# Cross attention over 12,544 keys on one NeuronCore: key splits shared with GpSimd, weights loaded later, and small sums taken off TensorE

## The reference, cut to what matters

```python
# x: (1, 128, 256), ctx: (1, 12544, 256), all fp32
h = layernorm(x)
Sim = (h @ w1)[:, None] + (ctx @ w2)[None, :] + (h * w3) @ ctx.T + b_sim     # 128 x 12544
hq_hat = softmax(Sim, axis=1) @ ctx                                          # 128 x 256
batt = softmax(max(Sim, axis=1), axis=0)                                     # over the 128 tokens
hc_bar = batt @ h                                                            # 256
x = x + concat([h, hq_hat, h * hq_hat, h * hc_bar]) @ W_qv + b_qv
x = x + linear_attention(layernorm(x), Wq, Wk, Wv, Wo, rope)                 # 16 heads, no softmax
x = x + sigmoid(shift_mix(ln(x)) @ W_r) * (relu(shift_mix(ln(x)) @ W_k) ** 2 @ W_v)
```

## Time and profile before

| what | value |
|---|---|
| median of 3 runs | 112.9 us (112.89 to 113.84) |
| the profiled execution's own time | 112.94 us |
| its span, first to last instruction | 111.2 us (1.74 us lie around it) |
| busy in the span | TensorE 105.4 us (95%), VectorE 93.6 (84%), ScalarE 81.3 (73%), GpSimd 26.2 (24%) |
| TensorE's share of the chain of waits | 91% |
| loads | 29.82 MB, nearly all on one queue |
| TensorE clock granted | full (2.4 GHz) in the whole span |

### The profile page before, as it was taken

How to read it: one execution, slowest core, us unless ns; L and a number is a source line. 1 busy time by engine, 2 the same in 40 slices (tenths; PEclk the granted TensorE clock), 3 DMA queues, 4 the chain that set the end, 5 groups by cost and what they waited for, 6 DMA issues and landing times.

```text
span 111.2 us, 1842 instructions
## 1 busy us (share of the span) xinstructions
PE 105.4 (95%) x580; PEld 85.2 (77%) x581; DVE 93.6 (84%) x153; ACT 81.3 (73%) x170; POOL 26.2 (24%) x44
## 2 busy tenths in 40 slices
PE   5899999999999999999999999999999998998890
PEld 2368777676757668888989999898989997887680
DVE  1488999989999999989999999999999846684342
ACT  5076755889979986999999899989986625903450
POOL 2239100000023334124242423367230000100100
PEclk9999999999999999999999999999999999999999
DMA  3999999999999999999999999950000000000001
GB/s 79 382 410 422 420 416 423 420 420 420 410 422 417 420 413 420 422 404 398 439 401 410 422 422 420 414 201 3 3 0 0 0 6 0 0 0 3 6 0 47
DMA packets 8220, 29.82 MB, mean 268 GB/s; under 512 B 1042, under 2 KB 1298, under 8 KB 8082
## 3 DMA queue, kind: packets, MB, share of 16 engines
q1 hardware_dynamic: 8064, 29.69, 66.0%
q10 hardware_dynamic: 146, 0.01, 0.1%
HBM read 29.57 MB, written 0.13 MB: 267 GB/s over the span
## 4 chain that ended last, share of the span: by engine, by line
PE 91%; DVE 2%; DMA 2%; issue 1%; ACT 1%; POOL 1%; DVEq 0%; POOLq 0%; ACTq 0%
PE mixed_ps L988 18%; PE scores_ps L959 10%; PE mixed_ps L990 9%; PE scores_ps L916 9%; PE scores_ps L945 8%; PE scores_ps L931 8%; PE scores_ps L935 8%; PE scores_ps L970 3%; DMA x_sb<-x_dram 2%; PE scores_ps L1081 2%; PE mixed_ps L1133 2%; PE side_ps L1007 1%; PE scores_ps L1146 1%; PE side_ps L1124 1%; PE scores_ps L1007 1%
## 5 line engine op out<-in xcount | busy, mean ns | idle before, releaser
L689 DVE TENSOR_TENSOR pair<-raw,pair 128x1024 fp32r<-128x1024 f32 (+1 forms) x41 | 49.4, 1220 | 1.4 <-ACT pair L486 1.4
L486 ACT ACTIVATE pair<-raw 128x512 fp32r<-128x512 f32 (+1 forms) x41 | 33.3, 814 | 6.6 <-DMA raw<-keys_dram 5.1
L988 PE MATMUL mixed_ps<-pair,turned_high 128*128 128x512 f32 x84 | 32.3, 418 | 0.0
L990 PE MATMUL mixed_ps<-pair,turned_low 128*128 128x256 f32 x84 | 23.6, 281 | 0.0
L461 POOL CAST pair<-raw 128x512 fp32r<-128x512 f32 x22 | 13.6, 618 | 27.2 <-DVE pair L689 23.9
L988 PEld LDWEIGHTS mixed_ps<-pair,turned_high 128*128 128x128 f32 x84 | 15.8, 188 | 2.8
L712 DVE TENSOR_SCALAR_CACHE_REDUCE neg_scores<-scores_ps,neg_max 128x1024 f32<-128x1024 f32 (+2 forms) x14 | 16.0, 1145 | 0.4
L518 ACT ACTIVATE turned_high<-scores_ps 128x512 fp32r<-128x512 f32 (+1 forms) x23 | 13.4, 584 | 3.9 <-PE scores_ps L959 3.9
L990 PEld LDWEIGHTS mixed_ps<-pair,turned_low 128*128 128x128 f32 x84 | 16.0, 190 | 0.0
L719 DVE TENSOR_TENSOR turned_low<-scores_ps,turned_high 128x512 fp32r<-128x512 f32 (+1 forms) x23 | 15.3, 669 | 0.2 <-ACT turned_high L518 0.2
L959 PE MATMUL scores_ps<-ident,neg_scores 128*128 128x128 f32 x98 | 14.6, 272 | 0.0
(11 more groups left out here) (189 smaller groups left out, 129.6 us busy)
## 6 DMA issues: line engine op xcount, KB each, us to landing
raw<-keys_dram SPq DMA_DIRECT2D x24, 512.0 KB, 10.6
raw<-rows_dram SPq DMA_DIRECT2D x24, 512.0 KB, 8.7
w<-weights_dram SPq DMA_DIRECT2D x1, 1792.0 KB, 9.5
w<-weights_dram SPq DMA_DIRECT2D x2, 512.0 KB, 11.5
const<-const_dram SPq DMA_DIRECT2D x1, 832.0 KB, 10.9
raw<-keys_last_dram SPq DMA_DIRECT2D x1, 256.0 KB, 9.5
raw<-rows_last_dram SPq DMA_DIRECT2D x1, 256.0 KB, 6.1
x_sb<-x_dram SPq DMA_DIRECT2D x1, 128.0 KB, 2.3
```

The source lines that it names most:

```text
L486: nc.scalar.activation(pair[:, use % PAIR_BUFS, 0, 0:columns], raw[:, slot(item), 0:columns], ACT.Copy)\
L689: nc.vector.tensor_tensor(out=pair[:, use % PAIR_BUFS, 1, 0:columns], in0=raw[:, slot(item), 0:columns], in1=pair[:, use % PAIR_BUFS, 0, 0 ...
L988: nc.tensor.matmul(mixed_ps[:, :].rearrange("p (h d) -> p h d", h=2), probs_high, both[:, :, t * D:(t + 1) * D], start=(k == EARLY and t = ...
L990: last = nc.tensor.matmul(mixed_ps[:, 0:D], probs_low, rows_tile(high, t), start=False, stop=(k == LATE - 1 and end))
```

## The change

It does the following.

1. Chunk 12 is no longer native, so it is split like the others. Six chunks are shared (10, 12, 14, 18, 20, 22), and in each GpSimd makes the low part of the last 448 of 1024 columns, VectorE that of the first 576.
2. The halves of W_qv are loaded behind chunks 12 and 18. The weight sums and the centring of blocks 0 to 3 come later in ScalarE's list; block 4 to 7's means and centring come after both `early_exp`, ahead of the first rows.
3. Chunks 22 and 23 are taken out of PSUM together.
4. h @ w1 + b_sim: GpSimd multiplies h by w1, loaded as rows (128 KB, behind chunk 13); ScalarE sums it behind the high part of chunk 19; VectorE adds b_sim where it takes the maximum. The three matmul instructions go.
5. Token attention: ScalarE takes the exponential of all 128 spread maxima in every partition and sums it; VectorE makes hc_bar with two multiply-and-sum instructions over 128 columns at k = 10. TensorE's three matmul instructions at k = 8 go.
6. The centred x is transposed by TensorE at the very start, copied out by ScalarE behind the high part of chunk 3, and added on VectorE together with the bias when x1 leaves PSUM, both halves on VectorE. The two instructions of L1065 go.

```diff
 EPS = 1e-5
-NATIVE = (0, 4, 8, 12, 16, 24)
-SHARED = (18, 20, 22)
+NATIVE = (0, 4, 8, 16, 24)
+SHARED = (10, 12, 14, 18, 20, 22)
+POOL_COLUMNS = 448
+W_BEHIND = (12, 18)
...
-    evictions = [(k, k + 1) for k in range(0, CHUNKS - 3, 2)] + [(k,) for k in range(CHUNKS - 3, CHUNKS)]
+    evictions = [(k, k + 1) for k in range(0, CHUNKS - 1, 2)] + [(CHUNKS - 1,)]
     EVICTIONS = len(evictions)
...
                 sp.dma_start(raw[:, slot(k), 0:width_of(k) * DH], src).then_inc(loaded[slot(k)], 16)
-                if k in (8, 11):
-                    part = (k - 8) // 3
+                if k in W_BEHIND:
+                    part = W_BEHIND.index(k)
                     sp.dma_start(w[:, 4 * part:4 * part + 4, :], blocks_in[:, 4 * part:4 * part + 4, :])\
                         .then_inc(w_qv_loaded[part], 16)
+                if k == 13:
+                    sp.dma_start(w1_rows[:, :], w1_rows_in).then_inc(w1_rows_loaded, 16)
             for k in range(CHUNKS):
...
                 use = split_before[k]
+                if k == 18:
+                    pool.wait_ge(low_done, split_before[15] + 1)
+                    pool.wait_ge(normed_done, DH)
+                    pool.wait_ge(w1_rows_loaded, 16)
+                    nc.gpsimd.tensor_tensor(out=hw1_parts, in0=normed[:, :], in1=w1_rows[:, 0:D], op=ALU.mult)\
+                        .then_inc(hw1_multiplied, 1)
                 pool.wait_ge(low_done, split_before[k - 1] + 1)
                 pool.wait_ge(high_done, use + 1)
-                nc.gpsimd.tensor_tensor(out=keys_part(pair[:, use % PAIR_BUFS, 1, :], k, DH - 1),
-                                        in0=keys_part(raw[:, slot(k), :], k, DH - 1),
-                                        in1=keys_part(pair[:, use % PAIR_BUFS, 0, :], k, DH - 1).bitcast(F32),
+                shared = slice(ITEM - POOL_COLUMNS, ITEM)
+                nc.gpsimd.tensor_tensor(out=pair[:, use % PAIR_BUFS, 1, shared], in0=raw[:, slot(k), shared],
+                                        in1=pair[:, use % PAIR_BUFS, 0, shared].bitcast(F32),
                                         op=ALU.subtract).then_inc(pool_low_done, 1)
...
                 act.wait_ge(x_neg_mean_done, 1)
-                nc.scalar.activation(x_c[:, :], x_sb[:, :], ACT.Identity, bias=x_neg_mean[:, :]).then_inc(x_c_done, 1)
-
+                nc.scalar.activation(x_c, x_sb[:, :], ACT.Identity, bias=x_neg_mean[:, :]).then_inc(x_c_done, 1)
+
+            center_x()
             act.wait_ge(q_done, DH)
...
                     keys_high(k)
-                if k == 8:
-                    center_x()
-                if k in (11, 12):
-                    weight_sum(2 * (k - 11))
-                    weight_sum(2 * (k - 11) + 1)
+                if k == 3:
+                    for a in range(DH):
+                        act.wait_ge(x_c_turned, a + 1)
+                        nc.scalar.activation(x_c_t[:, a, :], x_c_turn_ps[a], ACT.Copy).then_inc(x_c_t_done, 1)
+                if k == 19:
+                    act.wait_ge(hw1_multiplied, 1)
+                    nc.scalar.activation(hw1_parts, hw1_parts, ACT.Copy, accum_out=hw1_sum[:, :])\
+                        .then_inc(hw1_done, 1)
                 if k == 12:
+                    weight_sum(0)
+                    weight_sum(1)
+                if k == 13:
+                    weight_sum(2)
+                if k == 16:
+                    weight_sum(3)
                     weight_means(0)
-                if 13 <= k < 17:
-                    center(k - 13)
-                if 16 <= k < 20:
-                    weight_sum(k - 12)
-                if k == 20:
-                    weight_means(1)
-                    center(4)
-                if 20 < k < 24:
-                    center(k - 16)
+                    center(0)
+                    center(1)
+                if k == 17:
+                    center(2)
+                if k == 18:
+                    center(3)
+                    weight_sum(4)
+                    weight_sum(5)
+                if k in (20, 22):
+                    weight_sum(6 + (k - 20) // 2)
             for k in range(EARLY):
                 early_exp(k)
+            weight_means(1)
+            for block in range(4, 8):
+                center(block)
             rows_high(EARLY)
+            copy_early(0)
             rows_high(EARLY + 1)
-            for k in range(EARLY):
-                copy_early(k)
+            copy_early(1)
             act.wait_ge(max_done, EVICTIONS + 1)
...
                     act.wait_ge(batt_max_done, 1)
-                    nc.scalar.activation(batt[:, :], sim_max[:, :], ACT.Exp, bias=batt_neg_max[:, :])\
-                        .then_inc(batt_done, 1)
+                    nc.scalar.activation(batt_rows[:, :], batt_ps[:, 0:P], ACT.Exp, bias=batt_neg_max[:, :],
+                                         accum_out=batt_total[:, :]).then_inc(batt_done, 1)
                 if k == EARLY + 6:
...
-            act.wait_ge(b_kept_done, 1)
-            act.wait_ge(x1_projected, 1)
-            nc.scalar.activation(x1_t[:, 0, :], x1_ps[0], ACT.Identity, bias=b_c[:, 0, 0:1])\
-                .then_inc(x1_low_rows_done, 1)
-            nc.scalar.activation(x1_squared_t[:, 0, :], x1_ps[0], ACT.Square, bias=b_c[:, 0, 0:1])\
-                .then_inc(x1_low_squared, 1)
-            nc.scalar.activation(x1_kept_t[:, 0, :], x1_ps[0], ACT.Identity, bias=b_kept[:, 0:1])\
+            act.wait_ge(x1_low_rows_done, 1)
+            nc.scalar.activation(x1_squared_t[:, 0, :], x1_t[:, 0, :], ACT.Square).then_inc(x1_low_squared, 1)
+            nc.scalar.activation(x1_kept_t[:, 0, :], x1_t[:, 0, :], ACT.Identity, bias=b_c[:, 0, 1:2])\
                 .then_inc(x1_kept_done, 1)
             act.wait_ge(x1_high_rows_done, 1)
-            nc.scalar.activation(x1_kept_t[:, 1, :], x1_ps[1], ACT.Identity, bias=b_kept[:, 1:2])\
+            nc.scalar.activation(x1_kept_t[:, 1, :], x1_t[:, 1, :], ACT.Identity, bias=b_c[:, 1, 1:2])\
                 .then_inc(x1_kept_done, 1)
...
-                take_low(k, split_before[k], width_of(k) * (DH - 1 if k in SHARED else DH))
+                take_low(k, split_before[k], ITEM - POOL_COLUMNS if k in SHARED else width_of(k) * DH)
...
             dve.wait_ge(max_done, EVICTIONS + 1)
-            nc.vector.tensor_tensor(out=sim_max[:, :], in0=hw1_ps, in1=neg_max[:, EVICTIONS:EVICTIONS + 1],
-                                    op=ALU.subtract).then_inc(sim_max_done, 1)
+            nc.vector.scalar_tensor_tensor(sim_max[:, :], hw1_sum[:, :], w1_rows[:, D:D + 1],
+                                           neg_max[:, EVICTIONS:EVICTIONS + 1], ALU.add, ALU.subtract)\
+                .then_inc(sim_max_done, 1)
             rows_low(EARLY)
...
                 if k == EARLY + 8:
-                    dve.wait_ge(hc_bar_done, 1)
-                    nc.vector.reciprocal(batt_inv[:, :], batt_ps[:, DH:DH + 1]).then_inc(batt_inv_done, 1)
+                    dve.wait_ge(batt_done, 1)
+                    dve.wait_ge(normed_t_done, DH)
+                    nc.vector.reciprocal(batt_inv[:, :], batt_total[:, :]).then_inc(batt_inv_done, 1)
+                    for a in range(DH):
+                        if a > 0:
+                            dve.wait_ge(hc_bar_done, a)
+                        nc.vector.scalar_tensor_tensor(hc_parts[:, :], normed_t[:, a, :], 1.0, batt_rows[:, :],
+                                                       ALU.mult, ALU.mult, accum_out=hc_sum[:, a:a + 1])\
+                            .then_inc(hc_bar_done, 1)
+                    dve.wait_ge(hc_bar_done, DH)
                     dve.wait_ge(batt_inv_done, 1)
-                    nc.vector.tensor_scalar(hc_bar[:, :], batt_ps[:, 0:DH], batt_inv[:, :], None, ALU.mult)\
+                    nc.vector.tensor_scalar(hc_bar[:, :], hc_sum[:, :], batt_inv[:, :], None, ALU.mult)\
                         .then_inc(hc_bar_scaled, 1)
...
-            dve.wait_ge(x1_projected, 2)
-            nc.vector.tensor_scalar(x1_t[:, 1, :], x1_ps[1], b_c[:, 1, 0:1], None, ALU.add)\
-                .then_inc(x1_high_rows_done, 1)
+            dve.wait_ge(b_c_done, DH)
+            dve.wait_ge(x_c_t_done, DH)
+            for a, done in ((0, x1_low_rows_done), (1, x1_high_rows_done)):
+                dve.wait_ge(x1_projected, a + 1)
+                nc.vector.scalar_tensor_tensor(x1_t[:, a, :], x1_ps[a], b_c[:, a, 0:1], x_c_t[:, a, :],
+                                               ALU.add, ALU.add).then_inc(done, 1)
             dve.wait_ge(x1_high_rows_done, 1)
...
-            def features(kind, a, source, stop=False):
+            def features(kind, a, source, start=False, stop=False):
...
                     last = nc.tensor.matmul(x1_ps[o], w[:, kind * DH + a, o * P:(o + 1) * P], source[:, a, :],
-                                            start=False, stop=stop)
+                                            start=start, stop=stop)
                     if stop:
...
```

(26 more changed lines are left out.)

31 lines of the change are left out of this document (18 added, 13 removed).

## The result

The changed kernel takes 114.75 us (median of 17 runs, 114.12 to 117.41) where the kernel before took 113.53 us in the same session (17 runs, 112.89 to 115.17). The ratio is 1.0108, 95% interval 1.0077 to 1.0139: slower by 1.2 us. I had forecast 112.9 us and no change. The profiled execution of after took 114.75 us, its span is 112.9 us; it is at the median.

A forecast was written before the change was run, and what follows sets the result against it. It took TensorE and VectorE as balanced, with 0.25 us between them, and the loads as saturated: 112.94 + 0.83 - 0.25 - 0.30 - 0.30 = 112.92, called 112.9 us, no measurable change; range 111.1 to 114.1.

The forecast's parts named there:

- `exps(2)` 0.30 sooner: Between the phases: the row phase starts 0.3 us earlier, not the 1.2 VectorE saved; bounds -0.2 to +0.9.
- So work taken off TensorE counts only where VectorE and the loads let it go ahead.: Whole kernel: VectorE and loads are busy too, so TensorE's savings, 2.8 us at most, need not show.
- Rival A: Whole kernel: each of TensorE's savings is gained, 112.9 - 2.8 = 110.1 us, results 110 to 111.7; chance 0.12.
- A 512 KB item takes 1.25 us at 416 GB/s.: Key phase: saturated loads at the old rate; from chunk 19 on everything lands 0.3 us later.
- The stop: Key phase: chunk 19's load and the second W_qv half hold its high part until about 33.0, ending VectorE's 1 us lead.
- ScalarE's block: Between the phases: ScalarE's work from `early_exp` to `exps(2)` takes 5.3 us without a gap, ending at about 44.95.
- Rival B: Key phase: loads don't stop chunk 19, row phase starts 0.9 to 1.3 us earlier, 112.1 us; chance 0.25.
- Rival C: Between the phases: late W_qv half delays ScalarE's block, 113.9 us, or 114.2 with GpSimd's lock; chance 0.25.
- the block at k = 10: Row phase: VectorE's steps grow from 0.33 to 1.16 us, 0.83 more, between 0.7 and 1.2.
- 0.25 of lead: Row phase: VectorE is 0.25 us ahead of TensorE's need at k = 19, which absorbs that much of its added work.
- Tail, 0.3 less: Tail: about 0.2 us from TensorE's centred x and 0.1 from x1's first half; between 0.1 and 0.5.
- The three bounds: Range: lead between phases, VectorE's added work at k = 10 and tail at their bounds give 111.9 to 113.9 us.

The follow-up runs named there:

- r1: The changed kernel once more, nothing altered, beside the kernel before; ratio to before 1.0121.
- r3: The changed kernel with item 6 undone (centred x again as products with the identity); ratio to before 1.0029.
- r6: The changed kernel with items 5 and 6 both undone; ratio to before 0.9992.
- r9: The changed kernel with one more memset of one column on VectorE at 1.2 us; ratio to before 1.0088.
- r11: The changed kernel with the w1 rows loaded as 256 columns in place of 257; ratio to before 1.0096.
- r13: The kernel of items 1 to 3 with the w1 rows' load added, which nothing reads; ratio to before 1.0012.
- r15: The changed kernel with the w1 rows' load moved right behind x, ahead of chunk 0; ratio to before 1.0121.
- r7: The changed kernel with item 4 undone (h @ w1 back on TensorE, bias load back, no w1 rows); ratio to before 0.9999.
- r10: The changed kernel with items 4, 5 and 6 undone, so items 1 to 3 only; ratio to before 0.9899.
- r16: The kernel of items 1 to 3 without item 1, so items 2 and 3 only; ratio to before 0.9887.
- r18: The changed kernel with 32 bytes of padding putting the load ring back at byte 48896, and item 5 undone; ratio to before 0.9881.
- r5: The kernel before once more, nothing altered; one run, 113.51 us.
- r8: The kernel before with item 5 alone added; ratio to before 1.0077.
- r12: The kernel before with item 6 alone added; ratio to before 0.9993.
- r2: The changed kernel with item 5 undone (token attention's sums back on TensorE); ratio to before 1.0034.
- r17: The changed kernel with an unused 32-byte tile that puts the load ring back at byte 48896; ratio to before 0.9999.
- r4: The changed kernel with item 2 undone (W_qv behind chunks 8 and 11, ScalarE's old order); ratio to before 1.0211.

## Why the prediction was wrong, point by point

Of the error of 1.85 us (114.75 against 112.9), 0.6 is the base: I took 112.9 for the kernel before, the median of three runs, where 17 runs gave 113.53. The rest is the change. For the step from the profile before to the one after I had forecast `exps(2)` 0.30 sooner, it came 0.50 later; the row phase 0.58 longer, it was 0.92; the tail 0.30 shorter, it was 0.34 longer. So the largest miss lies ahead of `exps(2)`, where the loads rule, and the tail's is half the late step.

The account, from means over the profiles of the table. Placement: `exps(2)` starts at 45.69 in the ten kernels with item 2 and the ring moved (after, r1 to r3, r6, r9, r11, r13 to r15), at 44.70 in the five with item 2 and the ring in place (r7, r10, r16 to r18): +1.0 us. Single values of the two groups overlap (45.06 to 46.17 against 43.99 to 45.57), and three of the ten are those with the late first scores; without these three the mean is 45.57 and the step +0.9. Key phase with the ring in place: 44.70 against 45.35 without item 2 (before, r5, r8, r12): -0.65. Row phase: 46.37 with item 5 (ten kernels), 45.57 without it (ten; no value of one group reaches into the other): +0.8. VectorE's late step: +0.35. Tail: 0. Together +1.4 to +1.5; measured +1.2, with an interval of 0.9 to 1.6.

**"So work taken off TensorE counts only where VectorE and the loads let it go ahead."** Right. None of TensorE's savings show in the time, and r2 gives it back 0.64 us and gains 0.9. Rival A is out: no version comes near 110.1.

**Loads: "A 512 KB item takes 1.25 us at 416 GB/s."** This is the step that failed. It took the rate of before for the rate of after. At 408 GB/s an item takes 1.285 us, and that on some 25 items by the end of the key phase is about 0.9 us. I had costed what item 4 adds (0.3 us for the w1 rows) and not asked what the removal of a 4-byte tile does; r17, with 32 bytes put back, is 1.1% faster. Chunk 19's high part did start at 32.87, as forecast (near 33.0), but that was in part luck. In the ten kernels with item 2 and the ring moved it starts at 33.0 on average (32.33 to 33.77), in the five with the ring in place, whose rate I had reckoned with, at 32.6 (31.45 in r17 to 33.65 in r16). The stop is real in some (in r10 ScalarE waits 0.76 us for the second half of W_qv) and absent in others (in r17 nothing is waited for there). The loss grows behind it: chunk 23's high part starts at 38.95 on average with the ring moved, at 38.05 with it in place. ScalarE in r10, the wait and chunk 19's high part:

```profile
32.00 0.42 ACT L528 ACTIVATE w_sum_out<-w 128x256 f32<-128x256 f32 x1 [0.76 <-DMA w<-weights_dram]
...
33.22 1.06 ACT L488 ACTIVATE pair<-raw 128x1024 fp32r<-128x1024 f32 x1
```

**ScalarE's block, 5.3 us, `exps(2)` at about 44.95.** The block measured 45.79 - 40.03 = 5.76 in after, 0.17 of it a wait for a row chunk, and 44.31 - 38.86 = 5.45 in r17. The term was right within 0.15 where the loads run as before. The mark that I had set for "wrong", after 45.6, was met (45.79; r1, the same kernel, has 45.51), and it pointed at the loads and not at the block.

**Rival B, the lead of the key phase survives.** Its mechanism shows once the ring is in place: `exps(2)` is 0.65 us sooner on average, and about 1 us in r17. It was hidden under the placement in the kernels with the moved ring. As a case of this program it did not come about; as a reading of VectorE and the loads it was nearer than my own.

**Rival C, slower by ScalarE's block or a late second half of W_qv.** The side was right, the cause not: r4, which puts W_qv back, is 1.0 us slower still. In r10 ScalarE waits for that half for those 0.76 us, and r10 is fast all the same.

**Row phase: 0.83 more for the block at k = 10, less 0.25 of lead, less 0.30 at the start.** The block: forecast 1.16, measured 1.27 in after, 1.17 in r8. Its parts were otherwise than I had them. The second multiply-and-sum takes 0.71 in after in place of 0.27: the first has two SBUF inputs as well, and only the second has GpSimd's cast beside it. The Trainium skill (SBUF — State Buffer, "Who interferes with whom") has this as an exclusive lock of the shared ports, and the traces agree, here with 0.71 against 0.27 and in r2 with 1.65 against 1.21 for the same instruction without a cast beside it and 1.33 with only the end of one. I had the rule in the text and put its cost at the end of the bound only. The mean row phase says +0.80, nearly the whole length of the block's growth, so the 0.25 us of lead that I credited are hardly there. TensorE's idle time ahead of mix is 0.9 in the group, as forecast (0.5 to 1).

**Small terms.** The transposes at the start cost nothing in r12, as forecast (first scores at 5.89 us, before 6.13); that they lead to a slow start in some executions, as above, is open. GpSimd's 448 columns took 1.16 in the mean of six, forecast 1.14.

**Tail, 0.3 less.** From hq to the projection 0.13 went, the rest came back before vk; r12 says nothing gained. And then 0.35 us that no step of mine could hold: the late step at VectorE's 157 instructions. Four of these are item 5's, so item 5 in all costs some 1.15 us in this program (r17 against r18: 1.18% of 113.6 us, 1.3 us; by the medians at the full clock, 113.38 and 112.39, it is 1.0 us), where I had 0.83 less 0.25.

**Costed too low: item 2.** I gave items 2 and 3 no term of their own but the 0.3 us between the phases. r10 and r16 put them at 1.1 to 1.3 us, with r4 suggesting that most of it is item 2. Item 3 alone was not tried, so the split between the two is not shown. How r4 loses 1.0 us is not settled: its profile shows 0.4 of it, in the row phase. And of the 1.1 to 1.3 us the means over profiles find only the 0.65 ahead of `exps(2)`.

**Range.** The three bounds add up to 112.0 and 114.0, where I wrote 111.9 and 113.9; it changes nothing.

Open: why the rate falls with the placement, and whether 256 is the number (only two other offsets occur here, each 32 bytes off; 64 and 128 fit the three places as well). The Trainium skill (DMA: Bandwidth & Descriptors, "How a descriptor splits into AXI transactions") tells of reads in pieces of 256 bytes that must start at a multiple of 256, the unused bytes still costing beats (of 32 bytes). Here it is the side that is written that moved, so that the page covers this case is not shown. The direction would fit. By its count, as an estimate, a 4096-byte row would need 135 beats in place of 128 from byte 48864 (5.5% more) and 129 from 49952 (0.8%); measured are 408 against 419 GB/s, 2.7%, at both places, so the sizes do not follow it. Nor is it shown that VectorE's late step is a load of its code; the runs show only that it goes by the count.

## What to carry to other kernels

When a change adds or removes any tile, even of 4 bytes, compare the GB/s of a saturated stretch in both profiles first, and keep the buffers that large loads go into at a fixed address (here 48896 was fast, and 32 bytes off a multiple of 256 slow) by declaring them ahead of the small tiles. Work moved from an engine at 36.00 of 36 us to one at 35.9 costs nearly its full length there (here the row phase grew by 0.8 us for 0.84 to 0.94 us of work), and more where GpSimd reads SBUF beside it. An experiment that adds back the suspect is not enough (r13 said yes to the wrong cause): add the other half too, and ask whether the effect begins before its cause.

## What the hardware showed that I had not expected

- The DMA rate by place: 418 to 419 GB/s between 14 and 45 us in all nine programs whose ring begins at byte 48896 of a partition, 407 to 408 in all eleven whose ring begins at 48864 or 49952, on 512 KB loads of 4 KB per partition.
- VectorE starts one step 0.35 us late by its place in the stream of instructions: idle 1.35 us with 157 instructions in the program (eight profiles), 0.98 or 0.99 with 151 to 154, 156 or 158 (twelve).
- GpSimd's cast of 0.62 us stretches a VectorE instruction with two SBUF inputs from 0.27 to as much as 0.71 us.
- TensorE runs slower at the start in some executions of one kernel: the same two transposes of the normed input take 0.42 us each in after and 0.27 and 0.33 in r1, which is the same kernel, and the first scores start at 6.76 and 6.05 (5.89 in r12), with the same nine warm-up matmuls. It looks like a clock at its lower level, but the granted clock of these stretches reads 1.00 in all, so that is not shown.
- The loads' rate between 5 and 14 us is a matter of the execution: 389 GB/s in after and 404 in r1, the same kernel; 411 and 396 in before and r5.
